# Two mixture-of-experts stages: blocks of 256 rows with stationary weights, and 20 tiles routed ahead

## The reference

```python
x = x + 0.5 * ffn(layernorm(x), router_w, gate_w, up_w, down_w)
x = x + attn(layernorm(x), W_qkv, W_out)
x = x + 0.5 * ffn(layernorm(x), router_w, gate_w, up_w, down_w)
# ffn: logits = x @ router_w.T; the two largest, softmax over them; for each expert e
#   out += combine[:, e] * ((silu(x @ gate_w[e].T) * (x @ up_w[e].T)) @ down_w[e].T)
```

## Time and profile before

| | us |
|---|---|
| median of 3 runs (lowest, highest) | 1266.61 (1264.76, 1268.48) |
| the profiled execution | 1263.21 |
| its span in the profile | 1261.5 |
| first gather of the first loop; its last projection begins | 47.85; 252.65 |
| first gather of the second loop; its last scatter ends | 1027.55; 1239.65 |

### The profile page before, as it was taken

How to read it: one execution, slowest core, us unless ns; L and a number is a source line. 1 busy time by engine, 2 the same in 40 slices (tenths; PEclk the granted TensorE clock), 3 DMA queues, 4 the chain that set the end, 5 groups by cost and what they waited for, 6 DMA issues and landing times. The chain is left out here.

```text
span 1261.5 us, 28429 instructions
## 1 busy us (share of the span) xinstructions
PE 1196.3 (95%) x8838; PEld 912.5 (72%) x8838; DVE 905.5 (72%) x1995; ACT 791.4 (63%) x2264; POOL 814.1 (65%) x888
## 2 busy tenths in 40 slices
PE   7799999979999999999999999999999879999992
PEld 6588888856667666666667667766666668888881
DVE  6775344468888888888888997798998767533543
ACT  4665665656667666667667667767666656555552
POOL 4233356259888788788787787677666437666662
PEclk8899999989999999999999999999999969999996
DMA  9135122122221222122212222211221051113223
GB/s 323 32 96 155 57 56 70 42 69 56 62 53 42 60 60 50 44 60 54 57 46 51 62 64 51 60 43 43 52 49 37 18 184 43 47 50 113 62 63 110
DMA packets 87758, 86.54 MB, mean 69 GB/s; under 512 B 11248, under 2 KB 78704, under 8 KB 87232
## 3 DMA queue, kind: packets, MB, share of 16 engines
q1 hardware_dynamic: 76640, 65.50, 20.1%
q0 software_dynamic: 8864, 18.17, 5.2%
q10 hardware_dynamic: 2112, 1.05, 0.3%
HBM read 33.43 MB, written 17.69 MB: 41 GB/s over the span
## 5 line engine op out<-in xcount | busy, mean ns | idle before, releaser
L1915 POOL TENSOR_SCALAR at_prob<-at_prob,at_rec 128x128 f32<-128x128 f32 (+3 forms) x256 | 311.8, 1223 | 154.2 <-DVE at_rec L2126 152.3
L2306 ACT ACTIVATE at_prob<-at_s,at_nb 128x128 f32<-128x128 f32 (+3 forms) x512 | 264.7, 535 | 16.8 <-DVE at_nb L2118 13.4
L2317 ACT ACTIVATE at_probT<-at_pt 128x128 f32<-128x128 f32 (+3 forms) x256 | 105.2, 437 | 223.5 <-PE at_pt L2022 223.1
L790 POOL DMA_INDIRECT f_xb<-xn_dram,f_source x142 | 141.2, 994 | 160.4 <-PE f_b L1285 100.3
L2118 DVE TENSOR_REDUCE at_nb<-at_s 128x2 f32<-128x256 f32 (+3 forms) x256 | 203.5, 816 | 7.8 <-PE at_s L2008 7.8
L1447 DVE TENSOR_TENSOR f_hid<-f_b,f_silu 128x512 f32<-128x512 f32 x142 | 98.5, 693 | 135.8 <-PE f_b L1298 99.6
L2022 PE MATMUL at_pt<-ident,at_prob 128*128 128x128 f32 x1280 | 183.1, 275 | 5.5 <-DVE at_probT L2140 1.6
L2112 DVE TENSOR_TENSOR at_turned<-at_pj,rope 128x1024 f32<-128x1024 f32 x122 | 148.9, 1220 | 44.7 <-PE at_pj L1969 41.7
L2003 PE MATMUL at_s<-at_KT,at_QT 64*128 64x128 f32 (+3 forms) x1024 | 175.2, 460 | 5.2 <-DMA at_KT<-at_probT 2.8
L1909 POOL TENSOR_TENSOR at_R<-at_turned 128x512 f32<-128x512 f32 x126 | 157.4, 1268 | 24.0 <-DVE at_turned L2112 24.0
L2022 PEld LDWEIGHTS at_pt<-ident,at_prob 128*128 128x128 f32 x1280 | 140.9, 141 | 26.9 <-issue 15.5
(11 more groups left out here) (326 smaller groups left out, 2220.1 us busy)
## 6 DMA issues: line engine op xcount, KB each, us to landing
at_QT<-at_R SPq DMA_DIRECT2D x128, 128.0 KB, 2.4
at_KT<-at_R SPq DMA_DIRECT2D x124, 128.0 KB, 2.4
ys_dram<-y SPq DMA_DIRECT2D x71, 64.0 KB, 1.7
f_down<-down_t SPq DMA_DIRECT2D x2, 2048.0 KB, 9.3
xn_dram<-f_xn SPq DMA_DIRECT2D x12, 256.0 KB, 6.7
f_xb<-xn_dram,f_source POOLq DMA_INDIRECT x142, 2.5
X<-x SPq DMA_DIRECT2D x4, 512.0 KB, 6.2
gate<-gate_t SPq DMA_DIRECT2D x8, 256.0 KB, 5.1
```

The lines of the kernel that those rows point to most:

```text
L790: pool.indirect_dma_start(out=xb[j % AHEAD][:, :], out_offset=None, in_=xn_dram, in_offset=bass.IndirectOffsetOnAxis(ap=routing.source[:, ...
L1915: pool.tensor_scalar(w, w, rec[:, q, 1:2], None, ALU.mult).then_inc(probB_ready, 1)
L2306: act.activation(prob[q][:, h, :], s_bank[q % 2][:, h, 0:n], ACT.Exp, bias=nb[:, q, h:h + 1], scale=1.0, accum_out=sums[:, q, h:h + 1]).th ...
L2317: act.activation(probT[0][:, 0:q + 1, q * P:(q + 1) * P], pt_bank[0][:, at:at + (q + 1) * P].rearrange("p (b r) -> p b r", r=P), ACT.Copy) ...
```

## The change

- A block has 256 rows (`WIDE`), so there are 39 (2 x 32/2 + 7) instead of 71, or 78 columns of 128 rows. A block takes two gathers, and in the second loop two scatters, since an indirect DMA still moves 128 rows. y has three buffers of 256 rows instead of four of 128.
- The weights are stationary: 24 matmuls with 128 weight columns and the 256 rows of x moving give the hidden already transposed, so the four transposes of the hidden and ACT's copy of them go.
- `gate_up` is kept whole in fp32 in SBUF. For every block ACT copies its expert's 1024 columns as the high part and VectorE subtracts for the low part. The split ahead of the first loop, the store of up's low part and the reloads ahead of the second go.
- LEAD is 20; the attention takes a fifth leading group; three late groups are left for the phases and the end. The late lists are found at once at j = 9, and `numbered` of the late part moves from VectorE to GpSimd (j = 7, 8).
- After each of the four finds ahead of a loop TensorE does 12 unused transposes, and 20 before a loop.

```diff
+WIDE = 2
+OUTPUTS = 3
...
+        LEAD = 20
...
-        self.NB, self.E, self.lead, self.blocks = NB, E, LEAD, 2 * NB + E - 1
+        self.NB, self.E, self.lead, self.blocks = NB, E, LEAD, 2 * NB // WIDE + E - 1
+        self.columns = WIDE * self.blocks
...
         def gather(pool, j):
             pool.wait_ge(routing.lists_ready, routing.SOURCES[j >= SURE])
+            for t in range(WIDE):
+                c = WIDE * j + t
+                pool.indirect_dma_start(
+                    out=xb[j % AHEAD][:, t, :], out_offset=None, in_=xn_dram,
+                    in_offset=bass.IndirectOffsetOnAxis(ap=routing.source[:, c:c + 1], axis=0)
+                ).then_inc(xb_in[j % AHEAD], 16)
+
+        def keep_warm(pe, count):
+            for _ in range(count):
+                pe.transpose(bank[5][:, 0:P], ident[:, :], ident[:, :])
...
+                        for c in range(4):
+                            routing.find(pe, 0, c, found_bank)
+                            keep_warm(pe, 12)
...
-                        sp.dma_start(up[1][:, :, :].bitcast(F32), up_lo_dram).then_inc(up_lo_moved, 16)
...
-                        sp.dma_start(down[:, :, :, :], down_t).then_inc(down_in, 16)
...
                 for j in range(AHEAD):
                     gather(pool, j)
-                for j in range(BLOCKS + 3):
+                for j in range(BLOCKS + 2):
                     if j + AHEAD < BLOCKS:
                         pool.wait_ge(xt_psum, j + 1)
                         gather(pool, j + AHEAD)
+                    if j in NUMBERED_AT:
+                        routing.numbered(pool, 1, NUMBERED_AT[j])
...
+                    elif has(j, -2):
+                        scatter(j - 2)
...
+                def project(j):
+                    k = j % 2
                     pe.wait_ge(xlo_ready, j + 1)
+                    pe.wait_ge(wlo_ready, j + 1)
+                    x_hi, x_lo = xt[k][:, 0, :], xt[k][:, 1, :]
+                    for z in range(2):
+                        for g, into, reader in ((0, gate_bank[z], silu_ready), (1, up_bank[z], hid_ready)):
+                            wait(pe, reader, 2 * (j - 1) + z + 1)
+                            for c in range(2):
+                                cols = slice((2 * z + c) * P, (2 * z + c + 1) * P)
+                                o = into[:, c * ROWS:(c + 1) * ROWS]
+                                pe.matmul(o, w_hi[k][:, g, cols], x_hi, start=True, stop=False)
+                                pe.matmul(o, w_hi[k][:, g, cols], x_lo, start=False, stop=False)
+                                one = pe.matmul(o, w_lo[k][:, g, cols], x_hi, start=False, stop=True)
+                            one.then_inc(gu_psum, 1)
...
+                keep_warm(pe, 20)
+                for j in range(-1, BLOCKS + 1):
...
+                    if has(j, 0):
+                        project(j)
+                    if has(j, 1):
+                        turn_rows(j + 1)
...
+                    if has(j, -1):
+                        project_down(j - 1)
...
+                def leading_weights(j):
...
+                    e = owner(j)
+                    wait(act, gu_psum, 4 * (j - 2) + 4)
+                    act.activation(w_hi[j % 2][:, :, :],
+                                   gate_up[:, bass.ds(e, 1), :, :].rearrange("p a g f -> p (a g) f"),
+                                   ACT.Copy).then_inc(whi_ready, 1)
...
+                def output(j):
+                    r = j % OUTPUTS
+                    act.wait_ge(y_psum, j + 1)
+                    wait(act, y_out[r], STORED * (j // OUTPUTS))
+                    act.activation(y[r][:, :, :].rearrange("p t d -> p (t d)"), y_bank, ACT.Copy
+                                   ).then_inc(y_ready, 1)
...
+                def trailing_weights(j):
+                    e = owner(j)
+                    dve.wait_ge(whi_ready, j + 1)
+                    dve.tensor_tensor(w_lo[j % 2][:, :, :],
+                                      gate_up[:, bass.ds(e, 1), :, :].rearrange("p a g f -> p (a g) f"),
+                                      w_hi[j % 2][:, :, :].bitcast(F32), ALU.subtract).then_inc(wlo_ready, 1)
...
+                trailing_weights(0)
+                for j in range(-1, BLOCKS + 1):
+                    if has(j, 1) and j >= 0:
+                        trailing_weights(j + 1)
+                    if has(j, 0):
+                        hidden(j, 0)
+                    route_later(j)
...
+                    if has(j, 0):
+                        hidden(j, 1)
+                    if has(j, 1):
+                        trailing_rows(j + 1)
...
-        LEAD_NORMED = {LEAD_FACTORS + n: g for g, n in enumerate((5, 6, 8, 9))}
+        LEAD_NORMED = {LEAD_FACTORS + n: g for g, n in enumerate((5, 6, 8, 9, 10))}
```

More of the change, by code:

```diff
@@ L567, in join_found @@
     def join_found(self, dve):
[L569 to L572, removed]
+        link, later = self.link, self.later_found
+        first, stop = self.cols[1].start, self.cols[0].stop
+        old = self.found[:, :, first:stop]
+        link(dve.tensor_tensor(old, later[:, :, 0:stop - first], old, ALU.add))
+        link(dve.tensor_copy(self.found[:, :, stop:self.columns], later[:, :, stop - first:len(self.cols[1])]))
     def sources(self, dve, r):
@@ L592, in targets, with sevens, seven_owners @@
         dve.tensor_scalar(self.target[:, some], spot, -1.0, None, ALU.add).then_inc(self.lists_ready, 1)
+    def sevens(self):
+        first, sevens = 0, []
+        while first < self.blocks:
+            r = 0 if first < self.sure else 1
+            start = min(first, self.windows[r].stop - 1)
+            stop = min(start + 7, self.sure if r == 0 else self.blocks)
+            sevens.append((r, start, range(first, stop)))
+            first = stop
+        return sevens
+    def seven_owners(self, eng, r, start):
+        eng.wait_ge(self.lists_ready, self.OWNERS[r])
+        packed = eng.value_load(self.owners[0:1, start:start + 1], min_val=0, max_val=self.E ** 7 - 1)
+        return [packed // self.E ** d % self.E for d in range(7)]
     def owned(self, r):
@@ L747, in ffn @@
     WARM = 48
+    ROWS = WIDE * P
     with ExitStack() as ctx:
@@ L820, in ffn, with list_lead @@
             xts = [sb(f"xts{k}", [P, 512], ctx=early) for k in range(2)]
+            def list_lead(dve):
+                for k in range(2):
+                    routing.blocked(dve, 0, k)
+                for k in range(2):
+                    routing.numbered(dve, 0, k)
+                    for c in (2 * k, 2 * k + 1):
+                        routing.spots(dve, 0, c)
             if lead is None:
@@ L1083, in judge @@
                             one.then_inc(lg_psum, 1)
-                        def find(c):
-                            routing.find(pe, 0, c, bank[6][:, 0:2 * routing.most])
                         first = LEAD_GROUPS
@@ new lines, in project_down @@
+                def project_down(j):
+                    k, e = j % 2, owner(j)
+                    pe.wait_ge(hid_ready, 2 * j + 2)
+                    wait(pe, y_ready, j)
+                    if lead is None and j == 0:
+                        pe.wait_ge(down_in, 16)
+                    for t in range(WIDE):
+                        rows = slice(t * P, (t + 1) * P)
+                        for c in range(FC):
+                            one = pe.matmul(y_bank[:, rows], hidT[k][:, c, rows],
+                                            down[:, bass.ds(e, 1), c, :].rearrange("p a d -> p (a d)"),
+                                            start=(c == 0), stop=(c == FC - 1))
+                    one.then_inc(y_psum, 1)
```

656 lines of the change are left out of this document (277 added, 379 removed).

## The result

| | before | after |
|---|---|---|
| median of 4 runs, us | 1265.68 | 1295.47 (1291.06 to 1296.75) |
| ratio | | 1.0228 (95% interval 1.0194 to 1.0263) |
| span of the profiled execution | 1261.5 | 1294.8 |

A forecast was written before the change was run, and what follows sets the result against it. The prediction took TensorE to bound both loops before and GpSimd loop 2 after; terms -6, +3, +5, +1, -3 and +16 sum to +16 us on the profiled 1263.2, giving 1279 us, own range 1270 to 1293, widest 1252 to 1297.

The forecast's parts named there:

- the term that decides: Second loop: GpSimd becomes the bound with 156 DMAs at 1.28 us, and w_lo's subtraction holds them; +16 us.
- the sign of being right: Second loop: GpSimd without waits, one of four DMAs per block above 1.2 us, a pitch of 5.5 to 5.9 us.
- Loads are hidden: TensorE in the loops: weight loads lie beside the matmuls, so a 256-column matmul takes 0.116 us.
- The late routing: First loop: VectorE's routing in the first 13 blocks delays them; 7 us taken, bounds 0 and 20.
- The second phase: Between attention and second loop: longer list operations, and 12 transposes in front of the next find; +5 us, +2 to +6.2.
- The holds: Second loop: w_lo's subtraction on VectorE holds GpSimd's DMAs by 0.58 us per block, 23 us in all.
- The end: Second loop: some 2.6 us more where the last block drains.
- First phase: Ahead of the first loop: longer lists, a fifth group judged before them, transposes after finds, no weight-split wait; +3 us.
- Loop 1: First expert loop, bound by TensorE: 14.6 us saved by 4.8 us blocks, less a second gather and late routing; -6 us.
- Attention: In the attention: a fifth group is turned and judged on a TensorE that is busy 97%; +1 us, between 0 and 2.
- Tail: After the last scatter: three late groups instead of four are summed; -3 us.
- The rival without holds: Second loop: no DMA is held by w_lo's subtraction, so the loop takes 206 us and the whole 1257; chance 0.23.

The follow-up runs named there:

- the reduction: Changed kernel, second loop from the third block on: w_lo's subtraction replaced by a reduction of the same 1024 columns with one SBUF input; 1284.03 us (one run).
- the four pieces: Changed kernel, both loops: the subtraction that makes w_lo issued as four of 256 columns instead of one of 1024; 1288.45 us (one run).
- two edits here: Changed kernel, each alone: second loop's sums of the leading tiles three blocks later, 1290.03 us; the two moved list operations back on VectorE, 1292.45 us.

## Why the prediction was right and wrong

**Right: the mechanism of the term that decides.** GpSimd becomes the bound of loop 2 (its steady pitch is four times 1.28, and the blocks' mean pitch 5.65 us, where 5.5 to 5.9 was the sign of being right), and w_lo holds its DMAs; the reduction and the four pieces show it by 15.3 and 12.2 us. **The sentence of the Trainium skill's page "SBUF — State Buffer", section "Who interferes with whom", by which an instruction of VectorE with two inputs in SBUF contends with one of GpSimd that reads SBUF, holds here; its remark that tensor_tensor doesn't stall such DMAs does not: they last 1.97 us beside L1399 and 1.73 beside L538.** Loads are hidden at 0.119 us per matmul. The late routing costs loop 1 some 6.7 us (the first 12 pitches less 4.88 each, and less 1.7 for a first block at half clock); 7 was taken. The second phase came at 5.4 for 5: longer lists, and transposes in front of the next find.

**Right by luck: the size of loop 2,** +19.3 for +16. Its errors stood against each other. The holds are 15.4 and not 23, 0.40 us per block and not 0.58: w_lo's phase is not spread alike. In the five blocks from 1190.98 to 1211.49, for example, it begins 0.01 to 0.04 us after the start of a DMA, and no DMA there lasts over 1.0. The end costs 9.2 and not 2.6, because the last gathers leave TensorE four blocks behind; VectorE's wait for the sums, which the step did not look at, has a part in it that the runs do not size. And GpSimd waits 4.0 for the late list, a term that the step did not have.

**Wrong: the terms around it were mis-sized**, 17 us in all with loop 2 and all of one sign. The two that failed most are the first phase and the first loop, 9.5 us together. The measured time lies inside the widest range, 1252 to 1297, but outside the forecast's own, 1270 to 1293; the wide one reaches it by holds of nearly 1.1 us per block, which did not come.

- *First phase, +3, bounds 1 to 5.5; it measured 7.6.* What the step priced, longer lists and transposes, came at 2.5, from the first list operation to the first gather. What it gave no price to is the clock while the five groups are judged: 5.1 ahead of the lists, of which 4.4 are the half clock (26.64 against 22.25 where the full clock lasts). The statistics of 20 tiles come 1 us later than those of 16, the same warming ended at 12.07 instead of 13.66, and the first turn came only at 13.84. The removed split is not behind this, since it began at 20.87, when the last logits were under way. It did keep TensorE busy later: from 25 to 44 us for 17.4 of 19 us at full clock, now for 9.1 at half. What that costs the finds was not tried.
- *Loop 1, -6; it measured -1.1.* A block costs 4.88 instead of 4.8 (0.119 us per matmul for 0.116), so 11.3 are saved and not 14.6. The preparations for the attention, at blocks 34 to 37, cost 2.0 that the step left out; at the two dearest TensorE waits for x_lo, as in the routing. The first block at half clock, 1.7, was left out too. One bound of the step is added up wrong, without effect: at 0.113 the saving is 17 and not 18.
- *Attention, +1; 2.6.* Between the first and the last scores it takes 1.5 us longer, and the rest lies behind the last, where VectorE still does list operations of the leading tiles; that they are the cause is not shown.
- *Tail, -3; -0.4.* One group fewer is summed, but GpSimd's drain behind its last scatter takes 4.46 us in the trace for 2.98 before, and the first load is issued 6.2 us after the scatters' end instead of 4.8:

```profile
1279.62 3.25 SPq L1560 DMA_DIRECT2D f_got<-ys_dram  x6
1283.38 2.31 DVE L1585 SCALAR_TENSOR_TENSOR X<-f_got,wts,X 128x128 f32<-128x128 f32 x8 [10.54 <-DMA f_got<-ys_dram]
...
1287.85 4.19 DVE L1585 SCALAR_TENSOR_TENSOR X<-f_got,wts,X 128x128 f32<-128x128 f32 x8 [2.15 <-DMA f_got<-ys_dram]
```

The rival without holds (1257) was priced too low as well: the kernel with the reduction has hardly any, and takes 1284. Its loop is 220.9 where the sum gave 206, because the end and the list wait were missing from it; the rest is the terms outside the loop. What drain GpSimd needs after two scatters instead of one, and why, was not tried.

## What to carry to other kernels

When a change makes another engine the bound, don't price the stage by that engine's work alone: the old bound still rules the end, after the last item has been handed over, and every wait that is tied to the new bound's late results (here the sums' loads) comes to stand in front of something. Warming that is to bridge a wait has to last until the real work starts: here it ended 1.8 us short, and the phase ran at half clock. One run of a stage is not its time: two edits here seemed to gain 4 to 5 us in a loop that varies by 6 with the same code. And an operation of VectorE with two SBUF inputs beside a GpSimd that never rests is cheaper in small pieces.

## What was not expected of the hardware

- A 256-column matmul costs 0.119 us at full clock (granted 1.00 from 181.60 to 184.55) but 0.213 at half (0.50 from 61.20 to 66.10), so the clock gives a factor of 1.79 and not 2. Rows of PE in the first block, at half clock:

```profile
61.60 0.41 PE L1275 MATMUL f_b<-f_xt,f_w_lo 128*128 128x256 f32 x1
61.82 0.41 PE L1273 MATMUL f_b<-f_xt,f_w_hi 128*128 128x256 f32 x1
62.03 0.41 PE L1274 MATMUL f_b<-f_xt,f_w_hi 128*128 128x256 f32 x1
```

- The hold seems to work the other way too. In the kernel with w_lo in pieces, four pieces take 3.15 us instead of 1.42 beside GpSimd's list operation from 1088.01 to 1089.25 (DVE, then POOL); beside the second one, spots take 2.34 for 1.81:

```profile
1086.73 3.15 DVE L1401 TENSOR_TENSOR f_w_lo<-gate_up,f_w_hi 128x256 fp32r<-128x256 f32 x4
1093.07 1.42 DVE L1401 TENSOR_TENSOR f_w_lo<-gate_up,f_w_hi 128x256 fp32r<-128x256 f32 x4
```

```profile
1088.01 1.24 POOL L523 TENSOR_TENSOR f_named<-f_in_block,const_numbersb 128x624 bf16<-128x624 bf16 x1
```
